# Attention of a fused transformer kernel: from four to five stages, and the order of work in a step

## The reference, cut to what matters

```python
x = x + tanh(g_xattn[0]) * attention0(layernorm(x), ctx)
x = x + tanh(g_ffn[0])   * experts(layernorm(x))
x = x + tanh(g_xattn[1]) * attention1(layernorm(x), ctx)
x = x + tanh(g_ffn[1])   * ternary_ffn(layernorm(x))

# attention0: q, k rotated by position (rope), then
attn = softmax(einsum('bhqd,bhkd->bhqk', q, k) * scale)
out  = einsum('bhqk,bhkd->bhqd', attn, v) @ Wo + bo
# attention1: no rope; x and ctx normalised again with gain and bias,
#             y = heads(...) * sigmoid(qn @ Wg.T + bg), out = y @ Wo.T
```

## Time and profile before

| | |
|---|---|
| median of 3 runs | 3047.76 us |
| the profiled execution | 3043.93 us, its span 3042.1 us |
| attention of layer 0 | from the start to 786.6 us |
| experts | 789 to 1529 us |
| attention of layer 1 | 1529 to 2345 us |
| last feed-forward | from 2345 us |
| busy over the span | TensorE 66%, VectorE 58%, ScalarE 43%, GpSimd 33% |
| TensorE's granted clock, mean | 0.81 of full speed |

### The profile page before, as it was taken

One profiled execution on the slowest core, in us unless ns is written; L12 is line 12 of the kernel. 1 busy time (PEld: TensorE's weight loads), 2 busy tenths in 40 slices (PEclk: granted clock), 3 DMA queues, 4 the chain that ended last, 5 costly groups with the idle time before them and its releaser, 6 DMA issues. The chain is left out here.

```text
span 3042.1 us, 49795 instructions
## 1 busy us (share of the span) xinstructions
PE 2019.0 (66%) x14617; PEld 1560.7 (51%) x14617; DVE 1762.6 (58%) x3650; ACT 1315.4 (43%) x2345; POOL 1003.7 (33%) x1096
## 2 busy tenths in 40 slices
PE   5777677777543199999938788887886334444443
PEld 4555555555433199999825566665664222222222
DVE  5666666666454233333225555555553898988887
ACT  3444333344211044444324444444443566666665
POOL 0000100001266522222243333333330465565554
PEclk8988888888655599999968999999998566666666
DMA  2111111110443322222243333333331000000000
GB/s 68 40 36 43 36 39 36 37 43 26 141 154 125 123 76 87 87 87 87 77 82 65 69 80 71 69 68 67 76 70 56 17 27 28 28 21 28 28 25 17
DMA packets 177265, 185.56 MB, mean 61 GB/s; under 512 B 23745, under 2 KB 170946, under 8 KB 176130
## 3 DMA queue, kind: packets, MB, share of 16 engines
q1 hardware_dynamic: 152578, 149.49, 16.5%
q0 software_dynamic: 24576, 34.62, 5.6%
HBM read 109.82 MB, written 74.24 MB: 61 GB/s over the span
## 5 line engine op out<-in xcount | busy, mean ns | idle before, releaser
L527 DVE TENSOR_REDUCE a_mneg<-a_ps_s 128x8 f32<-128x960 f32 x256 | 285.8, 1151 | 63.0 <-PE a_ps_s L681 62.5
L681 PE MATMUL a_ps_s<-a_k,a_q 96*128 96x240 bf16 x1024 | 189.5, 334 | 153.9 <-DVE a_of L538 149.6
L377 ACT ACTIVATE a_probs<-a_ps_s 120x1024 f32<-120x1024 f32 x256 | 250.2, 1018 | 84.3 <-PE a_ps_s L695 84.3
L1295 DVE TENSOR_TENSOR e_h<-e_s,e_ps_ab 128x256 f32<-128x256 f32 (+1 forms) x213 | 89.4, 420 | 293.4 <-ACT e_s L1121 293.4
L1086 POOL TENSOR_TENSOR e_h_lo<-e_h 128x256 bf16<-128x256 f32 (+1 forms) x213 | 130.2, 611 | 326.0 <-DVE e_h L1295 326.0
L1314 PE MATMUL e_ps_ab<-e_xt_hi,e_w_hi 128*128 128x256 bf16 (+1 forms) x852 | 232.8, 273 | 0.1
L1314 PE MATMUL e_ps_ab<-e_xt_hi,e_w_lo 128*128 128x256 bf16 (+1 forms) x852 | 232.7, 273 | 0.0
L1314 PE MATMUL e_ps_ab<-e_xt_lo,e_w_hi 128*128 128x256 bf16 (+1 forms) x852 | 232.7, 273 | 0.0
L313 POOL TENSOR_TENSOR a_ve<-a_mv,a_eps 128x2 f32<-128x2 f32 x32 | 6.2, 195 | 664.7 <-DVE a_mv L506 664.7
L681 PEld LDWEIGHTS a_ps_s<-a_k,a_q 96*128 96x128 bf16 x1024 | 118.0, 121 | 195.2 <-DVE a_of L538 104.8
L341 POOL DMA_INDIRECT a_xa<-back_rows,a_where x128 | 202.2, 1580 | 45.8 <-issue 44.3
(11 more groups left out here) (237 smaller groups left out, 5430.8 us busy)
## 6 DMA issues: line engine op xcount, KB each, us to landing
e_xe<-sent_rows SPq DMA_DIRECT2D x71, 272.0 KB, 2.8
back_rows<-e_yo SPq DMA_DIRECT2D x71, 256.0 KB, 2.1
x_rows<-a_x SPq DMA_DIRECT2D x64, 256.0 KB, 3.2
a_xa<-in_x SPq DMA_DIRECT2D x32, 256.0 KB, 2.7
a_xr<-in_x SPq DMA_DIRECT2D x32, 256.0 KB, 2.9
e_xa<-x_rows SPq DMA_DIRECT2D x8, 1024.0 KB, 10.6
a_xa<-x_rows SPq DMA_DIRECT2D x32, 256.0 KB, 2.8
x_rows<-a_xa SPq DMA_DIRECT2D x32, 256.0 KB, 2.6
```

The source lines that it names most:

```text
L377: nc.scalar.activation(probs[0:S, 4 * g:4 * g + 4, :].rearrange("p h n -> p (h n)"), ps_s[0:S, g % 2, :, :].rearrange("p a n -> p (a n)"), ...
L527: nc.vector.tensor_reduce(mneg[:, g // 2, 8 * (g % 2):8 * (g % 2) + 8].rearrange("p (a h) -> p a h", a=2), ps_s[:, g % 2, :, 0:4 * S].rear ...
L681: last = nc.tensor.matmul(ps_s[:, g % 2, j // 2, (j % 2) * 2 * S:(j % 2 + 1) * 2 * S], q2[0:96, back.par, c, t * P:(t + 1) * P], k2[0:96, ...
```

## The change

Layer 0 now has five stages and layer 1 six: `back` is cut in two. `mid` takes the maxima (and in layer 1 the gate), `back` the scores, exponentials and products with the values, one step later. `ps_s` is cut into `ps_m` (two banks, for the maxima) and `ps_e` (two banks, for the rest), and the groups are halved: eight reductions of 4 heads in place of four of 8, eight exponentials of 512 columns in place of four of 1024. The turned-back result goes to `ps_t` and `ps_x`, each half divided for itself. The rows are turned at the end of the step ahead (`turn_rows`, into `ps_x`), and `xt` has two buffers. The normalisation moves from VectorE to GpSimd, the copy of half of the queries (`q2b`) from VectorE to ScalarE. In a step the projection of the rows comes first on TensorE, the rotation of queries early on VectorE, and the products with the values (`weigh`) ahead of the turning of the queries. The number of full steps falls by one in each layer, and that of partial ones at the ends rises by two.

```diff
-        xt = sb("xt", [P, KC, N], F32)
+        xt = sb("xt", [P, 2, KC, N], F32)
...
-        ps_s = psum("ps_s", [P, 2, 2, 512])
+        ps_m = psum("ps_m", [P, 2, 512])
+        ps_e = psum("ps_e", [P, 2, 512])
...
-                pipeline(eng, lambda *batches: step(None, *batches), 4, 6)
+                pipeline(eng, lambda *batches: step(None, *batches), 5, 6)
             else:
-                pipeline(eng, step, 5, 6)
+                pipeline(eng, step, 6, 8)
```

GpSimd's `norms`, new lines:

```diff
+                ng.wait(gp, pre, "rstd")
+                ne.wait(gp, pre.back(1), "xT")
+                if not first:
+                    fe.wait(gp, pre.back(1), "cT")
+                nc.gpsimd.tensor_tensor(ready[:, :], half[:, 0:1], half[:, 0:1], ALU.mult).then_inc(ng.sem, 1)
+                for t in range(NT):
+                    last = nc.gpsimd.tensor_scalar(xn[:, t, :], xa[:, p, t, :], mv[:, t, 0:1], rstd[:, t:t + 1],
+                                                   ALU.subtract, ALU.mult)
+                if not first:
+                    last = nc.gpsimd.tensor_scalar(cn[0:S, :], ca[0:S, p, :], mv[0:S, NT, 0:1], rstd[0:S, NT:NT + 1],
+                                                   ALU.subtract, ALU.mult)
```

Of TensorE, the waits that carry the prediction, and the order of a step:

```diff
+                def turn_back(i):
+                    if i == 0:
+                        ba.wait(pe, tail, "raw")
+                        da.wait(pe, back, "mT")
+                    else:
+                        if not first:
+                            da.wait(pe, back, "gate")
+                        if f:
+                            na.wait(pe, front, "x")
...
+                def turn_rows():
+                    ng.wait(pe, pre, "norm")
+                    if m and not first:
+                        da.wait(pe, mid, "gate")
...
+                    if i < 2:
+                        dv.wait(pe, mid.back(1), f"top{i + 6}")
+                    else:
+                        dv.wait(pe, mid, f"top{i - 2}")
...
+                if t:
+                    turn_back(0)
+                    turn_back(1)
                 if f:
...
+                    if not first:
+                        turn_context()
+                    project_rows()
                 if b:
                     scores(0)
                     scores(1)
+                if m:
+                    max_scores(0)
+                    max_scores(1)
                 if f:
+                    project_context()
+                for i in (2, 4):
+                    if b:
+                        scores(i)
+                        scores(i + 1)
+                    if m:
+                        max_scores(i)
+                        max_scores(i + 1)
+                if t:
+                    turn_result()
+                if b:
+                    scores(6)
+                    scores(7)
+                if m:
+                    max_scores(6)
+                    max_scores(7)
+                if f:
+                    turn_keys()
+                if t:
+                    project_result()
+                if b:
+                    weigh()
+                if f:
+                    turn_queries()
+                if m:
                     if not first:
...
+                        gate_rows()
+                    turn_maxima()
+                if pre is not None:
+                    turn_rows()
```

The order on VectorE:

```diff
+                if b:
+                    spread_maxima()
+                if m:
+                    top(0)
+                    top(1)
                 if n:
-                    statistics(pre)
-                if n:
-                    normalise(pre)
+                    statistics()
+                if f and first:
+                    rotate_queries()
+                if m:
+                    top(2)
+                    top(3)
+                if f and first:
+                    rotate_keys()
+                if t:
+                    divided(0)
+                    divided(1)
+                    if not first:
+                        gated()
+                if f:
+                    split_queries()
+                    split_keys()
+                if m:
+                    top(4)
+                    top(5)
+                if m:
+                    top(6)
+                    top(7)
+                    halves()
+                if f:
+                    key_columns()
+                if t:
+                    finish()
```

More of the change, by code:

```diff
@@ L255, in begin, with step @@
                 sp.dma_start(where[:, p, :], places[soon.n]).then_inc(w_ld[p], 16)
-            def step(soon, pre, front, back, tail):
+            def step(soon, pre, front, mid, back, tail):
                 if soon is not None and not first:
@@ L310, in norms @@
             def norms(pre):
-                nv.wait(gp, pre, "mean1" if first else "mean2")
+                p = pre.par
+                nv.wait(gp, pre, "mean")
                 if first:
@@ L708, in project_context @@
                         pe.wait_ge(c_ld[front.par], 16 * (front.half + 1))
+                        fa.wait(pe, front.back(1), "q2b")
                     else:
                         fa.wait(pe, front, "c")
[L711 removed]
                     context = ca[:, front.par, :, :] if first else ct
                     product(ps_kv[0:S, :], terms(context, slice(0, S), wkv, 0, 2 * D)).then_inc(fe.sem, 1)
[L715 to L720 removed]
@@ L721, in step @@
-                if b:
-                    max_scores(0)
-                    max_scores(1)
-                if f and not first:
-                    nv.wait(pe, front, "norm2")
-                    fv.wait(pe, front.back(1), "q2b")
-                    for c in range(KC):
-                        last = nc.tensor.transpose(ps_kv[:, c * S:(c + 1) * S], cn[0:S, c * P:(c + 1) * P], ident[0:S, 0:S])
-                    last.then_inc(fe.sem, 1)
-                if tail is not None:
-                    bv.wait(pe, tail, "o" if first else "gated")
-                    if f:
-                        fa.wait(pe, front.back(1), "k2a")
-                        fv.wait(pe, front.back(1), "k2b")
-                    transposed(ps_t, of if first else og).then_inc(te.sem, 1)
@@ new lines, in turn_result, with project_result, gate_rows @@
+                def turn_result():
+                    tv.wait(pe, tail, "o1" if first else "gated")
+                    transposed(ps_t, of if first else og).then_inc(te.sem, 1)
+                def project_result():
+                    ta.wait(pe, tail, "o")
+                    for i in range(NT):
+                        last = product(ps_x[:, i * D:(i + 1) * D], terms(ot, slice(i * P, (i + 1) * P), wo))
+                    last.then_inc(te.sem, 1)
+                def gate_rows():
+                    if t:
+                        tv.wait(pe, tail, "sum")
+                    elif f:
+                        na.wait(pe, front, "x")
+                    for i in range(NT):
+                        last = product(ps_x[:, i * D:(i + 1) * D], terms(xt[:, mid.par, :, :], slice(i * P, (i + 1) * P), wq, D) + bias_terms)
+                    last.then_inc(de.sem, 1)
@@ new lines, in turn_maxima @@
+                def turn_maxima():
+                    dv.wait(pe, mid, "m_lo")
+                    if f:
+                        fa.wait(pe, front, "k2a")
+                        fv.wait(pe, front, "k2b")
+                    elif t:
+                        ta.wait(pe, tail, "o")
+                    for i in range(NT):
+                        last = nc.tensor.transpose(ps_t[0:2 * H, i * P // 2:(i + 1) * P // 2].bitcast(BF16), mx[:, i, :], identb[:, :])
+                    last.then_inc(de.sem, 1)
@@ L767, in step @@
                     scores(1)
+                if m:
+                    max_scores(0)
+                    max_scores(1)
                 if f:
-                    if not first:
-                        if tail is not None:
-                            tv.wait(pe, tail, "sum")
-                        fa.wait(pe, front.back(1), "q2a")
-                        for t in range(NT):
-                            last = product(ps_x[:, t * D:(t + 1) * D],
-                                           terms(xt, slice(t * P, (t + 1) * P), wq, D)
-                                           + bias_terms)
-                        last.then_inc(fe.sem, 1)
@@ L778, in step @@
-                    fv.wait(pe, front, "k_lo")
-                    if b:
-                        ba.wait(pe, back, "mT")
-                    for c in range(NP):
-                        last = nc.tensor.transpose(ps_t[0:96, c * S // 2:(c + 1) * S // 2].bitcast(BF16), kx[0:S, c, :], identb[0:S, 0:S])
-                    last.then_inc(fe.sem, 1)
-                if b:
-                    scores(2)
-                    scores(3)
-                if f:
-                    fv.wait(pe, front, "q_lo")
-                    queries_transposed(ps_kv, NP // 2)
-                    if not first:
-                        fa.wait(pe, front, "gate")
```

(3 more changed lines are left out.)

497 lines of the change are left out of this document (243 added, 254 removed).

## The result

The changed kernel takes 3153.4 us (median of 4 runs, 3149.8 to 3160.7) against 3049.8 for the kernel before (4 runs on the same chip): ratio 1.0343, 95% interval 1.0317 to 1.0370. It is slower, as forecast, but by 104 us where 52 were forecast (3100 against the 3047.8 known then). The profiled execution took 3160.7 us, its span is 3158.9 us against 3042.1.

What follows compares the result with a forecast made beforehand. A chain of waits, not any engine's throughput, was taken to bound both layers' steps. 3043.93 us plus 47 in layer 0 and 8 in layer 1 gave 3099, predicted as 3100 us, range 3036 to 3165.

Steps and rivals of the forecast that it cites:

- +47: Layer 0: last `x1` at 833 us against 785.86, from a later first `x1` and steps of 25.2 us.
- -13: Layer 1, first to last `x1`: 718 us against 730.8; with +21 at the front, +8 in all.
- layer 1's chain: Layer 1's step at full clock, legs summed from the gate round to the turned queries: 23.3 us.
- +0.8 for the clock: Layer 1: one thin stretch of TensorE before its last maxima adds 0.8 us, making the step 24.1.
- 25.2 forecast: Step of layer 0: a chain of 23.2 us at full clock plus the clock's cost, against 23.86 before.
- 4.85 + 1.8 + 0.2: Layer 0: TensorE's last leg 4.85 us, half clock there +1.8, next step's projection of rows +0.2.
- signs named ahead: Layer 0: TensorE idle some 3 us before fifth scores, VectorE without gaps, clock below 0.80, result's projection at twice its length.
- Rival (b): Both layers' steps stay at 23.9 us and only the ends cost, +12 and +3: 3059 us; chance 0.17.
- Rival (c): Layer 0: VectorE stands for GpSimd's normalisations beside the rotation of queries, 0.7 to 1.2 us per step: 3125 us; chance 0.12.
- 0.65 and at most 1.3: Each normalisation moved to GpSimd takes 0.65 us, within 0.4 to 1.3, and costs nothing even at 1.3.
- Rival (a): Faster: the clock holds, mean about 0.95 in layer 0, steps 23.2 and 23.3 us: 3024 us; chance 0.13.
- Ends: One stage more delays the first `x1`: layer 0 at 91 us against 63.86, +27; layer 1's front +21.

Runs made afterwards that it cites:

- e1: Changed kernel with VectorE's `finish`, which writes `x1`, put ahead of `key_columns`: 3046.4 us, ratio 1.000 to the kernel before.
- e2: Changed kernel with ScalarE copying `k2a` ahead of the values, VectorE's order left alone: 3064.1 us, ratio 1.006 to the kernel before.
- e5: Changed kernel with four buffers for the values instead of two and a loop over four steps: 3076.6 us, ratio 1.010 to the kernel before.
- e3: Changed kernel with one added addition of 512 columns on VectorE behind the statistics: 3210 us (one run).
- e4: Changed kernel with two added additions of 512 columns on VectorE behind the statistics: 3298 us (one run).
- e13: e1 with seven additions of 512 columns on VectorE ahead of the sum for `x1`, in layer 1 only: 3103.6 us, ratio 1.019.
- e6: Changed kernel with both swaps, `x1` written ahead of the key columns and `k2a` copied ahead of the values: 3072.0 us, ratio 1.009.
- e12: Changed kernel, `x1` ahead of key columns; layer 0 also four value buffers, queries turned before value products, context projection behind group 3's maxima: 3011.2 us, ratio 0.987.
- e10: e1 with TensorE's projection of the context moved from ahead of scores 2 to behind the maxima of group 3: 3065.5 us, ratio 1.007.
- e8: Changed kernel with both swaps, four value buffers, and queries turned ahead of the result's projection and the value products: 3189.8 us, ratio 1.047.
- e14: e1 with eight additions of 512 columns on VectorE ahead of the sum for `x1`, in layer 1 only: 3097.4 us, ratio 1.017.

## Why the prediction was right or wrong

- **Sign, and where not.** Slower was right, and 3153 lies in the range, but both by luck: the forecast's mechanism wasn't what made it slower. It put the loss into layer 0 (+47, measured +13) and a gain into layer 1 (-13, measured +79). With the missed wait's path cut and all else as forecast, the kernel takes as long as before (e1, ratio 1.000), not 52 us more.
- **The failed step: layer 1's chain, "values 1.75, both turned queries 1.0", then the gate.** From the products' start to the gate's it has 2.75 us; measured are 4.79. It left out a wait that the code states: the values' copy waits for `pv` of two batches earlier, which after the cut of `back` is the same step's. I had followed the new waits and not the old ones whose distance in stages changed. Shown by e1 and e2, which cut what stands behind the wait (27.3 to 23.9), and by e5, which takes the wait away (24.8): there the leg is 2.79, as forecast. The missing 2.04 us are 1.43 by way of `x1` and about 0.6 by way of `ps_kv`, where the turned queries wait for the values' copy; e1 keeps the second part (3.36). With `x1` freed, the step of 23.9 is 0.2 from the forecast's 24.1.
- **Its size.** 1.4 us of wait cost 3.4 us of step; 1.7 are work at half clock, counted in busy time. The estimate "+0.8 for the clock" treated the falls as given for the step, while they depend on it.
- **Layer 0, 25.2 forecast, 23.9 measured, by its legs.** ScalarE, from the end of the first eight turned queries (408.74) to the turned-back result (412.50): 3.8, forecast 3.8. TensorE, to the first reduction (415.66): 3.2 against 3.1. VectorE, to the end of the sixth reduction (424.83 and half of 2.55): 10.4 against 11.4, the one leg that was 1 us off; overlaps of some 0.1 us between its instructions were missed, most in the divisions (1.35 against 1.6) and the splits (1.27 against 1.55). TensorE's last leg, what is left of 23.9: 6.5 against 4.85 + 1.8 + 0.2. Of the 1.65 above 4.85, 0.56 is the wait for the values' copy (row of 408.09), the missed wait again, so 1.1 is left to the clock: less than the 2.0 I took, since the half clock ended inside the result's projection (428.12). Of the signs named ahead, a granted clock below 0.80 (0.86) and a projection of twice its length (2.37) did not come; the wait of ScalarE, the pause of TensorE and VectorE without gaps did.
- **Rival (b), "the step stays at 23.9", 0.17,** was right for layer 0, and I gave it too little. Its reason has support, not proof: e3 and e4 (0.7 us: +1.7; 0.7 more: nothing), e5 (shorter leg, longer step), e13 (no wait left, +2.0 us). That VectorE's leg was 1 us shorter than my sum explains the same number in layer 0 alone, and may be all of it there; it doesn't explain e3, e4, e5 and e13.
- **Rival (c), VectorE stands for GpSimd's normalisation: not seen.** The last sum of the rotation beside it, now L605, took 0.69 us, as before (L606); the first product, L525, ends ahead of it and took 0.66 against 0.68. The lines of GpSimd, layer 0 and layer 1 (busy us, mean ns of one):

```profile
L335 POOL TENSOR_SCALAR a_xn<-a_xa,a_mv,a_rstd 128x256 f32<-128x256 f32 x52 | 75.5, 1459 | 0.0
```

```profile
L335 POOL TENSOR_SCALAR a_xn<-a_xa,a_mv,a_rstd 128x256 f32<-128x256 f32 x50 | 63.7, 1273 | 0.0
```

  I took 0.65 and at most 1.3; it is 1.46 and 1.27, so 256 columns cost GpSimd here as much as its addition of 512, 1.26. It had cover and cost nothing. The Trainium skill (GPSIMD Engine Reference, "Key points") has GpSimd contend for its SBUF interfaces with instructions of VectorE that have two SBUF inputs. Here it is GpSimd that pays: 1.46 beside the rotation against 1.27 in layer 1, and in e4, where the added additions keep their 0.67 us, one of GpSimd's instructions beside them takes 0.54 us (0.19 in the changed kernel):

```profile
2050.68 1.26 DVE L652 TENSOR_TENSOR a_idle<-a_idle 128x512 f32<-128x512 f32 x2
2050.85 0.54 POOL L324 TENSOR_TENSOR a_ve<-a_mv,a_oneeps 128x3 f32<-128x3 f32 x1 [16.30 <-DVE a_mv L593]
```

- **Rival (a)** fell: 0.86 in layer 0. **Ends:** first `x1` of layer 0 forecast 91, measured 95.9, front of layer 1 +21, measured +24.

## What to carry to other kernels

When a pipeline gets a stage more, go through every old wait whose distance is counted in batches: two buffers that were enough may now tie the front of a step to its back, and whatever is queued behind that wait inherits it. Follow such a wait through the queues of each engine, since here the harm was done two engines further on, and one swap of two lines took it away. Where the clock falls in every step, don't price a delay by its own length: measure it, because 0.7 us cost between nothing and 3.2 us here. And before calling a chain shorter, look in the new trace at what its next instruction waits for: the 1 us taken out in e2 and e6 came back as another wait.

## What the runs showed of the hardware

Steps that settle take few values: 22.1 or 22.2 (as pairs of 21.5 and 22.8, in e12 as groups of four), 23.9, 25.6 (as pairs), 27.3 and 30.7 us, in kernels with quite different work. Others (24.2, 24.8, 25.1, 25.9) are means over groups of unequal steps that repeat or wander. In each, the granted clock falls once or twice in most steps, and busy time of TensorE for the same instructions in layer 1 runs from 19.9 us a step (e10, clock 0.96) over 20.4 (e1, 0.93) to 22.2 (after, 0.88). That step and clock hold each other is my reading of this; why a step settles at one value and not at a neighbour, and why e8 or e14 don't, stays open, as no run here could fix the clock.
